# The causal mask of the latent attention as a select on GpSimd, with new orders of work for all engines

## The chip, the cores and the metric

The kernel runs on one core of one Trainium2 chip. The metric is the device time of one execution in microseconds. Before the change it is 1414.62 us, the median of three runs (1412.48 to 1416.68).

## What is computed

The input is 2 x 1024 x 128 (2048 tokens of width 128). The reference is a chain of residual layers; cut to what matters:

```python
x = x + 0.5 * moe0(layernorm(x))        # 8 experts, top 2, capacity, gelu
x = x + attn0(layernorm(x))             # 16 heads of 8, slope bias, causal softmax
x = x + 0.5 * moe0(layernorm(x))
x = x + 0.5 * latent_block(layernorm(x))
x = x + scan_block(layernorm(x))        # conv of 3, tanh, state scan, gelu ffn
x = x + 0.5 * latent_block(layernorm(x))

def latent_block(x):                    # inside: x + attention(rmsnorm(x)) + moe(rmsnorm(.))
    ...
    att = einsum(q, k) / sqrt(D)        # 16 heads of 64: 32 latent + 32 rotary columns
    mask = tril(ones((t, t)))
    att = where(mask, att, -inf)        # no weight on a later key
    att = softmax(att)
```

The change concerns this mask. A masked score becomes a weight of exactly zero after the exponential.

## The kernel before, in words

All tensors are held transposed, features or keys on the 128 partitions and tokens along the free dimension. There are five instruction streams (TensorE, ScalarE, VectorE, GpSimd and SyncE, which issues the DMAs), tied by semaphores, and the program has two large parts: `First` (the first expert layer and the first attention) and `Late` (the second expert layer, then the latent block, the scan block and the latent block again, each for batch element b = 0 and 1).

Attention goes by quads of four heads, n = 0 to 7 in `First` and 0 to 15 in `Late`, and in each quad by two phases ph of 512 queries. For each phase there are these tasks:

- `un` (TensorE, L1269, with the mask constant `maskA` at L1261) makes query-by-key scores, `red` (VectorE, L1544 to L1551) reduces them to row maxima; `m4`, `turn`, `ct` and the DMA `crow` put the maxima into a row of `QS`.
- `sc` (TensorE, `pe_scores`, L1283) makes key-by-query scores minus the maximum in a pair of PSUM banks, 128 keys by 512 queries for two heads at once, in steps listed in `SCORES`. The last five steps of a phase touch the diagonal (`masked`); there, for each piece, two halves of two matmuls (L1290) add -1e30 from the constants `idA` and `maskB` on the diagonal square.
- `exp` (ScalarE, L1461) writes the exponentials of one step, 128 x 1024, into `PR`, a ring of `NPR = 4` group buffers. Two steps make a group; a group is one or two key blocks (`group_pieces`) by four heads.
- `pv` (TensorE, L1383) multiplies a group with the values; it waits for the group's last exponential and frees its buffer for the group four later.
- `ev`, `den`, `ln`, `rx` (ScalarE and VectorE), `on` (GpSimd, L1592) and `proj` (TensorE) normalise and project.

Operands of a later quad are built between the scores: `bld` (TensorE, L1249 to L1251), `bt` (VectorE, L2139), the shuffle `swp` (L2148), the rotation's sums and split `rot` (GpSimd, L2317, L2318, L2320, as one task; quads 0 and 8 do it on the other engines), and a DMA `put`. Norms, routing and experts of a finished half, and for b = 0 also its scan block (the convolution `cv` at L2227 and L2233, products `pct`, `psg`, `pbt` on GpSimd, the scan `scn`), run among the quads of the other half.

The order on each engine is worked out when the program is built. `Plan.simulate` walks through time; whenever an engine is free it takes, among the ready heads of its streams, the task of lowest priority value (`ORDER` for four engines, `WISH` weights for TensorE), charges it `COST`, and notes the order. It also gives out the PSUM banks. What comes out is five fixed lists; on the chip each engine goes through its list and waits on semaphores. So a cost or a weight changes no instruction, only its place and its bank.

Of the kernel before, what the change touches and what calls it, by code (L numbers as in the profile page):

```python
# [102 lines left out]
class Plan:  # L103
# [8 lines left out]
    COST = {"turn": 0.2, "proj": 1.9, "m4": 0.25, "ct": 0.27, "crow": 1.2, "den": 0.72, "ev": 0.58, "ln": 0.63,  # L112
            "rx": 0.63, "on": 1.27, "add": 0.68, "qk": 1.75, "qkh": 1.02, "qkl": 1.22, "val": 1.9, "vc": 1.02, "vs": 0.5,
            "put": 7.0, "egb": 2.7, "exh": 0.6, "exl": 0.69, "ewh": 0.68, "ewl": 0.69, "eu": 1.28, "eg": 0.68, "eh": 0.75,
            "et": 1.3, "ed": 0.87, "eup": 0.75, "mean": 0.87, "cen": 0.69, "sq": 0.63, "var": 0.87, "vln": 0.65, "vex": 0.63,
# [4 lines left out]
    ORDER = {"ACT": ("eg", "rxp", "exh", "ewh", "cmc", "vex", "qkh", "vc", "ev", "exp", "rx", "ln", "vln", "sq"),  # L120
             "DVE": ("ro", "exl", "ewl", "eup", "cen", "eh", "scl", "ct", "m4", "add", "qkl", "red", "den"),
             "POOL": ("vs", "et", "on"),
             "SP": ("crow", "gd", "put", "egb")}

    WISH = {"scm": 2, "unm": 2, "leadm": 4, "upm": 2, "bldm": 2, "sc": 2, "sc1": 1, "un0": 1.9, "un2": 2.89,
# [17 lines left out]
    def quad(self, n, units, values, first_add=(None, None)):  # L143

        add = self.add
        for ph in range(2):
# [8 lines left out]
            for i in range(len(SCORES[ph])):  # L155
# [7 lines left out]
                need = [x]  # L163
# [166 lines left out]
    def simulate(self):  # L330
# [11 lines left out]
        pending = []  # L342
        t = 0.0
        while left:
# [4 lines left out]
            for e in engines:  # L349
# [105 lines left out]
class Late(Plan):  # L455
# [8 lines left out]
        "ve0": 0.63, "scb": 0.49, "ff": 1.27, "xqh": 0.6, "xql": 1.3, "wqh": 1.2, "wql": 1.4, "key": 0.87, "km": 1.4,  # L464
# [51 lines left out]
    @staticmethod  # L516
    def turned(n):
        return ("rotl", n) if n in FAST else ("rot", n)
# [1985 lines left out]
```

## Time and profile before

| | |
|---|---|
| median of three runs | 1414.62 us |
| the profiled execution's own time | 1418.79 us |
| its span, first to last instruction | 1417.0 us |
| TensorE, VectorE | 94%, 71% of the span busy |
| ScalarE, GpSimd | 62%, 28% |
| mean granted clock of TensorE | 0.982 |

The profile is of one execution. The busy time of an engine is the union of its instructions; matmul ends are modelled, so overlapping matmuls count once and the last one's drain counts in full. PE is TensorE, PEld its weight loads, DVE VectorE, ACT ScalarE, POOL GpSimd, SP SyncE. The stages are: load and first expert layer to about 200 us, first attention to 425, second expert layer to 595, the latent and scan blocks to 1417.

### The profile page before, as it was taken

To read this page: it belongs to the slowest core of one execution; us is meant where nothing else is said; L and a number is where in the kernel's file an instruction comes from. 1 tells how busy PE (TensorE), PEld (TensorE's weight loads), DVE (VectorE), ACT (ScalarE), POOL (GpSimd) and SP (SyncE) were. 2 spreads that over 40 slices of the span, in tenths; PEclk is the share of its full clock that TensorE was granted. 3 is DMA by queue.
4 is the path that set the end of the run, shared out by engine and by line. 5 is a ranking of instruction groups with operands and counts; after the bars stand their busy time and mean duration, and the time that the engine had idled before them with its cause. 6 is when DMAs were issued, how large, how long until landed. Compare 5 with 4: busy or idle time off the path is not lost.

```text
span 1417.0 us, 27150 instructions
## 1 busy us (share of the span) xinstructions
PE 1325.2 (94%) x10934; PEld 565.5 (40%) x10934; DVE 1010.7 (71%) x1554; ACT 876.9 (62%) x1124; POOL 394.6 (28%) x317
## 2 busy tenths in 40 slices
PE   7999998989889999989999998989998999999997
PEld 6444333333334444343444343433432334433443
DVE  5444778899915447789887977688878697977635
ACT  5344347788774553366666867766777576675672
POOL 4554420101112555452220332021305033202010
PEclk9999999999999999999999999999998999999998
DMA  6633101000003631011111010010010101101100
GB/s 168 130 61 71 30 9 35 13 2 2 1 1 72 164 60 34 9 24 24 35 24 23 2 24 7 18 35 17 8 23 1 24 12 24 31 8 24 24 2 15
DMA packets 31876, 45.80 MB, mean 32 GB/s; under 512 B 5941, under 2 KB 12789, under 8 KB 31701
## 3 DMA queue, kind: packets, MB, share of 16 engines
q1 hardware_dynamic: 31752, 44.08, 14.7%
q8 instruction: 87, 1.43, 0.4%
q14 instruction: 37, 0.30, 0.1%
HBM read 25.39 MB, written 1.18 MB: 19 GB/s over the span
## 4 chain that ended last, share of the span: by engine, by line
PE 75%; DVE 11%; ACT 8%; issue 4%; DMA 1%; POOL 1%; SPq 0%; ACTq 0%; DVEq 0%; POOLq 0%
PE ps L1283 13%; PE ps L1383 12%; PE ps L1328 8%; ACT PR L1461 6%; PE ps L1249 6%; PE ps L1269 5%; PE ps L1250 5%; PE ps L1251 5%; DVE BM L1551 3%; PE ps L1880 2%; PE ps L1261 2%; PE ps L1347 2%; PE ps L1290 2%; PE ps L1394 2%; PE ps L1395 1%
## 5 line engine op out<-in xcount | busy, mean ns | idle before, releaser
L1461 ACT ACTIVATE PR<-ps 128x1024 f32<-128x1024 f32 x432 | 431.4, 1027 | 204.1 <-PE ps L1290 133.5
L1551 DVE TENSOR_REDUCE BM<-ps 128x2 f32<-128x1024 f32 (+2 forms) x384 | 350.6, 950 | 52.1 <-PE ps L1269 50.7
L1283 PE MATMUL ps<-QS,KS 48*128 48x512 f16 (+7 forms) x2688 | 306.6, 329 | 28.6 <-ACT PR L1461 21.8
L1383 PE MATMUL ps<-PR,VS 128*32 128x512 f32 (+3 forms) x2304 | 232.1, 499 | 2.2 <-ACT PR L1461 1.7
L1283 PEld LDWEIGHTS ps<-QS,KS 48*128 48x128 f16 (+1 forms) x2688 | 108.7, 95 | 199.1 <-ACT PR L1461 87.5
L1269 PE MATMUL ps<-KS,QS 48*128 48x128 f16 (+2 forms) x1728 | 162.6, 274 | 19.0 <-DVE BM L1551 10.9
L1544 DVE TENSOR_REDUCE BM<-ps 128x8 f32<-128x1024 f32 x96 | 116.8, 1220 | 38.7 <-PE ps L1269 37.9
L1269 PEld LDWEIGHTS ps<-KS,QS 48*128 48x128 f16 x1728 | 68.8, 95 | 136.4 <-issue 50.2
L1592 POOL TENSOR_TENSOR OS<-OS,RX 128x512 f32<-128x512 f32 x24 | 31.8, 1327 | 266.9 <-ACT RX L1477 266.9
L1592 POOL TENSOR_TENSOR ON<-OS,RX 128x512 f32<-128x512 f32 x24 | 32.5, 1354 | 260.2 <-ACT RX L1477 260.2
L1249 PE MATMUL ps<-YA,QS 128*128 128x512 f16 x256 | 99.6, 389 | 0.2
L1250 PE MATMUL ps<-YA,QS 128*128 128x512 f16 x256 | 99.3, 388 | 0.0
L1251 PE MATMUL ps<-YA,QS 128*128 128x512 f16 x256 | 99.1, 387 | 0.0
L1418 ACT ACTIVATE BT<-ps 128x512 f32<-128x512 f32 x64 | 38.2, 597 | 95.3 <-PE ps L1251 95.2
L1290 PE MATMUL ps<-maskB,idA 64*128 64x64 bf16 (+1 forms) x1536 | 91.3, 202 | 0.0
L1418 ACT ACTIVATE HL<-ps 128x512 f32<-128x512 f32 x64 | 37.5, 597 | 81.2 <-PE ps L1251 81.1
L1383 PEld LDWEIGHTS ps<-PR,VS 128*32 128x32 f32 x2304 | 53.2, 109 | 80.9 <-issue 63.2
L1290 PEld LDWEIGHTS ps<-maskB,idA 64*128 64x128 bf16 x1536 | 70.3, 94 | 32.8
L1586 POOL TENSOR_TENSOR HL<-HL,PR 128x512 f32<-128x512 f32 x46 | 58.7, 1290 | 57.7 <-DVE HL L1510 45.8
L1547 DVE TENSOR_REDUCE BM<-ps 128x4 f32<-128x1024 f32 x48 | 58.4, 1217 | 6.4 <-PE ps L1269 6.3
L2317 POOL TENSOR_TENSOR KS<-BT,HL 128x1024 f16<-128x1024 f32 x14 | 33.1, 2363 | 87.3 <-DVE HL L2148 87.3
L1261 PE MATMUL ps<-maskA,idA 64*128 64x256 bf16 (+1 forms) x384 | 48.5, 331 | 9.0 <-DVE BM L1551 7.0
(300 smaller groups left out, 2062.0 us busy)
## 6 DMA issues: line engine op xcount, KB each, us to landing
PR<-gates SPq DMA_DIRECT2D x32, 512.0 KB, 13.2
QS<-KS SPq DMA_DIRECT2D x64, 128.0 KB
QS<-KS SPq DMA_DIRECT2D x64, 64.0 KB
WM<-W_in SPq DMA_DIRECT2D x1, 2048.0 KB, 11.7
QS<-HL SPq DMA_DIRECT2D x48, 32.0 KB
KS<-HL SPq DMA_DIRECT2D x48, 32.0 KB
QS<-CT SPq DMA_DIRECT2D x96, 2.0 KB
PR<-x SPq DMA_DIRECT2D x4, 256.0 KB, 4.2
```

The costliest lines, as they stand in the source:

```text
L1249: pe.matmul(dst, w[0], x[0], start=True, stop=False)
L1250: pe.matmul(dst, w[1], x[0], start=False, stop=False)
L1251: return pe.matmul(dst, w[0], x[1], start=False, stop=True)
L1261: pe.matmul(ps[pair][:, w, :].rearrange("p (i c) -> p i c", c=P)[:, :, at_:P], idA[rows, half, :], maskA[rows, half, at_:P].unsqueeze(1).t ...
L1269: ins = pe.matmul(ps[pair][:, w, off:off + nk * P], QS[rows, sl, qt * P:(qt + 1) * P], KS[rows, ks, k0 * P:(k0 + nk) * P], start=not diag, ...
L1283: ins = pe.matmul(ps[pair][:, w, off:off + cols], KS[rows, ks, kt * P:(kt + 1) * P], QS[rows, qs, (ph + 1) * TT - cols:(ph + 1) * TT], sta ...
L1290: ins = pe.matmul(ps[pair][:, w, off:off + wide], idA[rows, half, :], maskB[rows, half, 0:wide], start=False, stop=(half == 1))
L1328: pe.matmul(single(plan, ("ed", 16 * t)), w_out[:, i // 2, i % 2, :], ring_he(lat, u), start=(i == 0), stop=(i == 15)).then_inc(sig["ed"], 1)
L1383: ins = pe.matmul(dst[32 * j:32 * j + 32, TT - cols:TT], v, PR[:, buf, j, off:off + cols], start=(g == 0), stop=(g == NGRP[ph] - 1))
L1461: act.activation(dst, src, ACT.Exp, scale=0.125 if lat else 1.0).then_inc(sig["exp"], 1)
L1544: ins = dve.tensor_reduce(BM[:, ph, p, :, :, 0], bnk[:, :, :].rearrange("a w (i c) -> a w i c", c=P), AX.X, ALU.max)
L1551: ins = dve.tensor_reduce(BM[:, ph, p, :, qt - 4 * ph, part], bnk[:, :, off:off + nk * P], AX.X, ALU.max)
```

## The change

The mask constants stay in use for `First` and for the unit scores. In `Late` the matmuls of L1290 are not issued; instead a new GpSimd task `mk` sets the weights of later keys in the diagonal squares of a masked group to zero, in place in `PR`, and `pv` of such a group waits for it in place of the exponential. The rotation on GpSimd becomes three tasks of one instruction. The plan learns of a port that all GpSimd tasks and the VectorE tasks named in `PORT` pass one after the other. Costs, ranks and weights of both plans are replaced.

```diff
@@ class Plan, costs and weights (First uses these)
-    COST = {... "m4": 0.25, ... "ewh": 0.68, "ewl": 0.69, "eu": 1.28, "eg": 0.68, "eh": 0.75, ... "eup": 0.75,
+    COST = {... "m4": 0.2, ... "ewh": 0.62, "ewl": 0.66, "eu": 1.3, "eg": 0.61, "eh": 0.69, ... "eup": 0.69,
+    PORT = {"exl", "ewl", "scl", "gwl", "mup", "krot", "krl"}
-             "POOL": ("vs", "et", "on"),
+             "POOL": ("et", "on", "vs"),
-    WISH = {... "leadm": 4, ... "un2": 2.89, "qk": -0.24, "vl": 1.91, "proj": 3.84, "bldf": 0.9, "up": 2.16 ...}
+    WISH = {... "leadm": 6, ... "un2": 2.85, "qk": 0.38, "vl": 1.75, "proj": 2.96, "bldf": 0.72, "up": 0.52 ...}
@@ Plan.quad
-                need = [x]
+                cut = self.LATENT and masked(ph, g)
+                need = [add("POOL", "mk", ("mk", n, ph, g), x) if cut else x]
@@ Plan.cost
-                return ((0.66 if self.LATENT else 0.23)
-                        + 0.08 * len(steps) * masked(task[2], group_of_step(*task[2:4])))
+                return 0.66 if self.LATENT else 0.23 + 0.08 * len(steps) * masked(task[2], group_of_step(*task[2:4]))
+        if kind == "mk":
+            return 0.66 * len(group_pieces(*task[2:4]))
@@ Plan.simulate
+                if e == "POOL" or (e == "DVE" and task[0] in self.PORT):
+                    c += max(0.0, port - t)
+                    port = t + c
@@ class Late, costs and weights (all ranks of ORDER are new too)
-        "ksw": ... "bt": 1.22, "rot": 7.0, "lg": 1.1, "dn": 4.9, "cv": 1.3, "dts": 0.9, "scn": 2.3
+        "ksw": ... "bt": 1.22, "rot": 2.36, "lg": 0.98, "dn": 4.6, "cv": 1.95, "dts": 0.68, "scn": 2.4
-             "POOL": ("et", "psg", "pct", "pbt", "xl", "on", "ff", "rot", "xql"),
+             "POOL": ("mk", "pct", "on", "mk", "pbt", "rot", "ff", "xql", "et", "xl", "psg"),
-    WISH = {"scm": 2, "leadm": 4, "upm": 2, "bldm": 2, "un2": 2.1, "lead": 2, "pv3": 2.5, "pv": 3.61, "qk": 0.71,
-            "vl": 1.9, "proj": 3.06, "mean": 1, "bldf": 0.8, "bld2": 3.31, "bld": 1.8, "up": 1.7, "dn": 1.22, ...}
+    WISH = {"scm": 3, "leadm": 3, "upm": 3, "bldm": 3, "un2": 2.39, "lead": 4, "pv3": 0.82, "pv": 2.84, "qk": -1.92,
+            "vl": 8.18, "proj": 9.87, "mean": -0.05, "bldf": -2.69, "bld2": 3.15, "bld": 2.15, "up": -0.36, "dn": 2.88, ...}
@@ Late.builds
-            r = add("POOL", "rot", ("rot", n), r, old)
+            for j in range(3):
+                r = add("POOL", "rot", ("rot", n, j), r, old)
@@ pe_scores
-            diag = masked(ph, group_of_step(ph, i))
+            diag = masked(ph, group_of_step(ph, i)) and not lat
@@ pe_attn, pv
-                pe.wait_ge(sig["exp"], c("exp", n, ph, min(2 * g + 1, LASTS[ph])))
+                if lat and masked(ph, g):
+                    pe.wait_ge(sig["mk"], c("mk", n, ph, g))
+                else:
+                    pe.wait_ge(sig["exp"], c("exp", n, ph, min(2 * g + 1, LASTS[ph])))
@@ pool_attn
+            if task[0] == "mk":
+                n, ph, g = task[1:]
+                pool.wait_ge(sig["exp"], c("exp", n, ph, min(2 * g + 1, LASTS[ph])))
+                for _, off, _ in group_pieces(ph, g):
+                    square = PR[:, group(n, ph, g) % NPR, :, off:off + P]
+                    ins = pool.affine_select(out=square, in_=square, compare_op=ALU.is_ge, fill=0.0, base=0,
+                                             pattern=[[0, QUAD], [1, P]], channel_multiplier=-1)
+                ins.then_inc(sig["mk"], 1)
+                return
```

The second convolution cost of `Late.cost` goes from 1.2 to 1.9. The three instructions of the rotation and their waits are the same as before.

## Rows read from the trace of the kernel before

**Rows 1.** The page, part 1: busy us, share of the span, instructions.

```profile
PE 1325.2 (94%) x10934; PEld 565.5 (40%) x10934; DVE 1010.7 (71%) x1554; ACT 876.9 (62%) x1124; POOL 394.6 (28%) x317
```

**Rows 2.** Windows: length; PE, PEld, DVE, ACT, POOL busy; clock, DMA, GB/s.

```profile
200.00:425.00 225.00, 200.98 (x2305) 78.79 (x2301) 175.12 (x230) 176.00 (x211) 23.18 (x24) 0.98 0.04 9
425.00:595.00 170.00, 166.76 (x667) 73.51 (x667) 93.92 (x143) 73.09 (x111) 86.14 (x69) 0.98 0.32 69
595.00:1417.00 822.00, 765.85 (x7135) 321.25 (x7133) 631.87 (x985) 547.03 (x670) 188.71 (x111) 0.98 0.09 19
595.00:810.00 215.00, 203.04 (x2053) 86.37 (x2052) 182.73 (x285) 145.06 (x180) 60.13 (x34) 0.98 0.11 23
810.00:880.00 70.00, 63.41 (x532) 24.30 (x526) 54.60 (x67) 49.14 (x59) 21.70 (x13) 0.93 0.06 13
1050.00:1120.00 70.00, 63.09 (x498) 24.08 (x496) 50.05 (x61) 50.60 (x62) 21.72 (x12) 0.90 0.09 18
```

**Rows 3.** The chain of waits, 595 to 1377 us: its share by line.

```profile
by line: PE ps L1283 20.4%; PE ps L1383 14.1%; ACT PR L1461 6.0%; PE ps L1269 5.7%; issue 4.6%; DVE BM L1551 3.9%; PE ps L1880 3.0%; PE ps L1249 2.5%; PE ps L1290 2.5%; PE ps L1347 2.2%; PE ps L1261 2.2%; PE ps L1250 2.2%; PE ps L1251 2.1%;
```

**Rows 4.** Waits of PE, 595 to 1377 us: sum us, times, longest.

```profile
PE ps L1283 <- ACT PR L1461: 11.2, 20, 1.1
...
PE ps L1261 <- DVE BM L1551: 6.4, 3, 2.9
```

**Rows 5.** Window 595 to 1417 us of the mask matmuls (L1290) alone.

```profile
595.00:1417.00 822.00, 63.68 (x1024) 47.01 (x1024) 0.98 0.09 19
```

**Rows 6.** Timeline of one diagonal stretch: start us, length us, engine, line.

```profile
1337.90 0.25 PE L1290 MATMUL ps<-maskB,idA 64*128 64x64 bf16 x4
...
1337.98 0.38 PE L1269 MATMUL ps<-KS,QS 48*128 48x512 f16 x2
...
1342.16 0.25 PE L1290 MATMUL ps<-maskB,idA 64*128 64x64 bf16 x4
...
1342.25 0.33 PE L1283 MATMUL ps<-QS,KS 49*128 49x128 f16 x6
...
1342.71 1.02 ACT L1461 ACTIVATE PR<-ps 128x1024 f32<-128x1024 f32 x1 [1.35 <-PE ps L1290]
...
1344.87 1.02 ACT L1461 ACTIVATE PR<-ps 128x1024 f32<-128x1024 f32 x1 [1.13 <-PE ps L1290]
...
1345.19 1.07 PE L1383 MATMUL ps<-PR,VS 128*32 128x384 f32 x16
...
1347.25 0.64 PE L1383 MATMUL ps<-PR,VS 128*32 128x256 f32 x8
```

**Rows 7.** Groups of POOL by form: busy us, mean ns, idle before.

```profile
L2318 POOL TENSOR_TENSOR BT<-BT,HL 128x1024 f32<-128x1024 f32 x14 | 34.8, 2488 | 0.0
L2317 POOL TENSOR_TENSOR KS<-BT,HL 128x1024 f16<-128x1024 f32 x14 | 33.1, 2363 | 87.3 <-DVE HL L2148 87.3
...
L2320 POOL TENSOR_TENSOR KS<-BT,KS 128x1024 f16<-128x1024 f32 x14 | 31.5, 2251 | 1.1
...
L949 POOL TENSOR_SCALAR_AFFINE_SELECT pick<-pick 24x512 bf16<-24x512 bf16 x3 | 2.0, 651 | 0.4
...
L937 POOL TENSOR_SCALAR_AFFINE_SELECT maskB<-maskB 64x256 bf16<-64x256 bf16 x2 | 0.8, 406 | 0.0
```

**Rows 8.** Groups of DVE by form, 595 to 1417 us.

```profile
L2233 DVE SCALAR_TENSOR_TENSOR QS<-QS,colp 128x1023 f32<-128x1023 f32 x4 | 8.4, 2091 | 0.0
...
L2264 DVE SCALAR_TENSOR_TENSOR QS<-QS,colp 128x1024 f32<-128x1024 f32 x2 | 2.5, 1274 | 0.0
```

**Rows 9.** Source view of L1592 (ns min/median/max), timeline of 840 to 850.

```profile
L1592 POOL TENSOR_TENSOR ON<-OS,RX x24: 1264/1274/2241, 216.8 to 1353.7; 128x512 f32<-128x512 f32 x24
...
843.54 2.24 DVE L2233 SCALAR_TENSOR_TENSOR QS<-QS,colp 128x1023 f32<-128x1023 f32 x1
...
844.78 2.98 POOL L2320 TENSOR_TENSOR KS<-BT,KS 128x1024 f16<-128x1024 f32 x1
...
847.72 2.24 POOL L1592 TENSOR_TENSOR ON<-OS,RX 128x512 f32<-128x512 f32 x1
```

More of the change, by code:

```diff
@@ L111 @@
     SINGLES = (4, 5, 6, 7)
-    COST = {"turn": 0.2, "proj": 1.9, "m4": 0.25, "ct": 0.27, "crow": 1.2, "den": 0.72, "ev": 0.58, "ln": 0.63,
+    COST = {"turn": 0.2, "proj": 1.9, "m4": 0.2, "ct": 0.27, "crow": 1.2, "den": 0.72, "ev": 0.58, "ln": 0.63,
             "rx": 0.63, "on": 1.27, "add": 0.68, "qk": 1.75, "qkh": 1.02, "qkl": 1.22, "val": 1.9, "vc": 1.02, "vs": 0.5,
-            "put": 7.0, "egb": 2.7, "exh": 0.6, "exl": 0.69, "ewh": 0.68, "ewl": 0.69, "eu": 1.28, "eg": 0.68, "eh": 0.75,
-            "et": 1.3, "ed": 0.87, "eup": 0.75, "mean": 0.87, "cen": 0.69, "sq": 0.63, "var": 0.87, "vln": 0.65, "vex": 0.63,
+            "put": 7.0, "egb": 2.7, "exh": 0.6, "exl": 0.69, "ewh": 0.62, "ewl": 0.66, "eu": 1.3, "eg": 0.61, "eh": 0.69,
+            "et": 1.3, "ed": 0.87, "eup": 0.69, "mean": 0.87, "cen": 0.69, "sq": 0.63, "var": 0.87, "vln": 0.65, "vex": 0.63,
             "scl": 0.75, "rlg": 4.6, "ro": 0.34, "rxp": 0.31, "rrk": 0.8, "rtp": 0.48, "gd": 0.4, "cmc": 0.6, "cmp": 2.0}
@@ L341, in simulate @@
         left = len(self.needs)
-        pending = []
+        pending, port = [], 0.0
         t = 0.0
@@ L484 @@
-    WISH = {"scm": 2, "unm": 2, "leadm": 4, "upm": 2, "bldm": 2, "sc": 2, "sc1": 1.02, "un0": 1.9, "un2": 2.1,
-            "lead": 2, "un1": 1, "une": 1, "pv3": 2.5, "ahead": 3, "pv": 3.61, "qk": 0.71, "vl": 1.9, "proj":
-            3.06, "ed": 1.1, "mean": 1, "eu": 1.2, "eu1": 0.3, "mode": 0.4, "bldf": 0.8, "bld2": 3.31, "bld":
-            1.8, "up": 1.7, "dn": 1.22, "short": 1}
+    ORDER = {"ACT": ("ev", "eg", "sq", "roth", "krh", "vln", "ewh", "rxp", "sg", "kh", "vex", "si", "ge", "exh", "vc",
+                     "dx", "rex", "exp", "dl", "ve0", "lath", "th", "ab", "ln", "xp", "xh", "de", "xqh", "gwh", "wqh",
+                     "rx"),
+             "DVE": ("ro", "exl", "eh", "gtc", "scl", "den", "cen", "ct", "ewl", "scb", "hf", "krot", "m4", "rt", "eup",
+                     "cv", "dt0", "gt", "mup", "bd", "kl", "oup", "st3", "mya", "cp", "bt", "krl", "wql", "rotl", "dts",
+                     "latl", "fup", "ksw", "swp", "scn", "km", "st2", "add", "rotd", "red", "fya", "gwl"),
+             "POOL": ("mk", "pct", "on", "mk", "pbt", "rot", "ff", "xql", "et", "xl", "psg"),
+             "SP": ("wl2", "egb", "wl1", "crow", "put", "gd", "st", "kput")}
@@ L489, in build @@
+    WISH = {"scm": 3, "unm": 2, "leadm": 3, "upm": 3, "bldm": 3, "sc": 2.04, "sc1": 1.24, "un0": 1.98, "un2":
+            2.39, "lead": 4, "un1": 1.05, "une": 1.17, "pv3": 0.82, "ahead": 3, "pv": 2.84, "qk": -1.92, "vl":
+            8.18, "proj": 9.87, "ed": 1, "mean": -0.05, "eu": 1.13, "eu1": 0.05, "mode": 0.46, "bldf": -2.69,
+            "bld2": 3.15, "bld": 2.15, "up": -0.36, "dn": 2.88, "short": -0.61}
     def build(self):
@@ L2311, in pool_late @@
                 elif kind == "rot":
[L2312 to L2314 removed]
+                    n, j = args
                     b0 = BT[:, 0:2, :]
                     hi, lo = two(STG[:, 0, :]), two(STG[:, 1, :])
[L2317 to L2320 removed]
+                    if j == 0:
+                        pool.wait_ge(sig["swp"], c("swp", n))
+                        put_landed(pool, n - 1)
+                        pool.tensor_tensor(hi, b0, BS, ALU.add).then_inc(sig["rot"], 1)
+                    elif j == 1:
+                        pool.tensor_tensor(b0, b0, BS, ALU.add).then_inc(sig["rot"], 1)
+                    else:
+                        pool.wait_ge(sig["rot"], c("rot", n, 1))
+                        pool.tensor_tensor(lo, b0, hi, ALU.subtract).then_inc(sig["rot"], 1)
                 elif kind == "pct":
```

36 lines of the change are left out of this document (11 added, 25 removed), and 14 rows, old and new, of tables (COST, WISH).

## The prediction

> **What bounds the kernel now.** I read first the page's engine line [rows 1]: TensorE is busy for 1325.2 of 1417.0 us, VectorE for 71%, ScalarE for 62%, GpSimd for 28%. TensorE is the bound on average, so I cut the span into stages [rows 2]. The edit to the computation lives in the latent stage, 595 to 1417 us. There TensorE is busy for 765.85 of 822 us, so it has 56.1 us of idle time; in the first attention (200 to 425) it has 24.0. GpSimd is busy for 188.7 us of the latent stage, 23%. The two 70 us stretches that hold the scan work have a granted clock of 0.93 and 0.90, so part of each ran at 1.2 GHz instead of 2.4.
>
> The chain of waits over 595 to 1377 [rows 3] says what of TensorE is on the path. The mask matmuls (L1290) hold 2.5% of these 782 us, 19.6 us; the scores before them 20.4%, the value products 14.1%, ScalarE's exponentials 6.0%, VectorE's big reductions 3.9%. TensorE's own waits in the stretch [rows 4] are small: 11.2 us for the exponentials, 6.4 for reductions ahead of a unit.
>
> **Part 1, the latent mask matmuls go.** Each latent quad has two phases, each with 8 diagonal pieces (1, 1, 2, 2 and 2 in the last five steps), and a piece has four matmuls: 16 quads x 16 x 4 = 1024, the count of the latent row [rows 5]. That row gives 63.68 us of busy time, 0.25 us a piece, but this counts the modelled drain of each matmul, which the next one overlaps. The timeline [rows 6] has the pace: a mask group starts at 1337.90 and the next work at 1337.98, then 1342.16 to 1342.25. So a piece delays what follows by 0.09 us, and 256 x 0.09 = 23.0 us. The bounds are 19.6 (all that the chain shows) and 63.7 (the whole busy union). I take the pace, since the starts are what the engine gives, and of its 23.0 the 19.6 that were on the path. The rest sits where VectorE or ScalarE came last.
>
> **Part 2, the selects on GpSimd.** Three groups of each phase are masked, with 1, 2 and 1 pieces, so 4 selects over 4 heads x 128 columns: 32 phases x 4 = 128 instructions in 96 tasks. No select of 128x512 f32 is in the trace. Selects of 256 and 512 elements a partition took 406 and 651 ns [rows 7], though the longer is on 24 partitions only. The upper bound is a two-operand step of 128x512, 1.27 us (L1592's median [rows 9]). I take 0.65, the nearest in size and kind; then 83 us are added, and GpSimd is at about 272 of 822 us, 33%. At 1.27 it would be 163 more, 43%. Either way it is no throughput bound; it matters by latency alone.
>
> The latency: the value product (pv) of a masked group now waits for the select, not for the exponential, and on the in-order TensorE everything planned after it waits too. Cover can be read off the timeline [rows 6]. The exponential of the second step of the two-piece group ran 1342.71 to 1343.73, and its pv started at 1345.19: 1.46 us of slack, against 2 x 0.65 = 1.30 plus a hand-over. For the last group the exponential ended at 1345.89 and pv began at 1347.25: 1.36 against 0.65. So even the old order nearly covers it, by the scores and units of the next step; the new plan knows the 0.66 and can put pv later. If cover is gone everywhere, the price is the whole 83 us; if it is perfect, nothing. A second thing is queued behind pv: the exponential of the group four later needs the buffer that it frees; ScalarE has idle time, so a microsecond more there is covered. I take 2 us in all for uncovered selects in the steady run, and 1 us at the very end, where after the last quad's last exponential (about 1371) nothing is left to put ahead of pv. The first half (b = 0) of a layer ends while the other half's quads run, so there it is covered.
>
> **Part 3, GpSimd's queue.** In 14 of 16 quads the rotation occupies it with three steps of 2.36, 2.49 and 2.25 us [rows 7]. Before, they were one task; the edit makes them three of unchanged work, so that a select can be planned between. A select can still come due just as one starts: 42 steps, at worst 2.4 us each, 101 us; at best none, because the plan looks ahead. With 96 tasks in 822 us and 99 us of rotation, chance alone would put 12 selects behind one, with 1.2 us of mean wait, 14 us, less the slack above of at least 0.1 to 0.7. I take 3. The put DMA waits for the third step as before; a select between delays it by 0.65 to 1.3, and a quad's operands are built more than a quad ahead, so that costs nothing; without this cover it would be 14 x 1.3 = 18 us.
>
> There are shared turns too. VectorE's convolution steps with both operands in SBUF took 2.09 us, against 1.27 for a step of equal size with the same kind of operands [rows 8], and beside one of them, begun at 843.54, GpSimd's L2320 took 2.98 instead of a mean of 2.25 [rows 7], and the L1592 behind it 2.24 instead of 1.27 [rows 9]. So the two engines hold each other up when each reads SBUF so. A select is such work; most of VectorE's time is reductions out of PSUM, which went at their 1.22 us regardless. Eight large convolution or scan steps and the few scalings could each catch one: at best nothing, at worst about 20 x 1.3 = 26 us, and I take 2. The Trainium skill (SBUF — State Buffer, the section on two separate sides) says that it is an exclusive lock: whichever starts first blocks the other for the whole instruction. By that rule a select next to a 2 us convolution waits for its end; the trace agrees in kind. The sum changes by nothing, as the stretches in which both occur are 140 of 822 us. The Trainium skill also speaks against the placement (GPSIMD Engine Reference, performance versus the Vector engine): a tight one-input loop over 512 elements takes 769 ns there. By its price the selects would be 98 us instead of 83, and 1.5 for a two-piece group is just over its slack; the trace has 651 ns for 512 elements, and the measured number is the one used.
>
> **Part 4, the plans.** Both orders are made anew: costs near what the trace shows (rotation 3 x 2.36, the convolution 1.95 and 1.9 instead of 1.3 and 1.2), a port that GpSimd and VectorE's listed steps pass one at a time, new ranks and weights. In the latent plan the weights change a lot (three score pairs at once instead of two; projection and values far later); in the first plan little. No row prices an order. What it can give back is TensorE's idle time, 56.1 and 24.0 us, and the lost clock; what it can cost has the same size, as the old order had 11.2 us of waits for exponentials that a poor one would multiply. I take 7 of gain in the latent stage (an eighth of its idle time, mostly around the scans, whose old costs were furthest off) and 1 in the first attention. The expert stages (425 to 595) have TensorE at 98%, so nothing.
>
> **The sum**, against the profiled execution: -19.6 + 3 + 3 + 2 - 8 = -19.6 us. The execution took 1418.79 us (span 1417.0 and 1.8 around it), which is 4.2 above the median 1414.62. So 1399.2 profiled, and 1395 as the median.
>
> **Rivals.** B, the new order gives much: half of the latent and first idle time (40 us), so -19.6 + 8 - 40 = -52, 1363, with a middle at -40, 1375. For it: the old costs missed the scan by a factor of 1.6, and TensorE waited 2.9 us once for a reduction late on VectorE [rows 4]. Against it: most gaps are under 1 us, which no order removes. C, TensorE wasn't last: VectorE is at 182.73 of 215 us in the first latent stretch (85%), and the saved time turns into waits for its reductions. Then about 8 of 19.6 is left and costs of 8 eat it, 1408 to 1416. Against it: over all of 595 to 1377 the chain has VectorE's reductions at 3.9% only. D, on the slower side: selects are late at pv. Place: pv of masked groups, behind a rotation step, or after a select of 1.27 us. Price: up to 83 us of latency. It decides when more than 22.6 of 83 us (the 19.6 and the 8 of the plans, less 5 for queue and turns) show on TensorE, 0.24 us a task; with half exposed the time is 41.5 - 22.6 = 19 longer, 1434. TensorE's waits would also cut its granted clock, as in the scan stretches. Against it: the slack of 1.36 to 1.46 us. E, the change doesn't do what it says, for instance by selects so slow that they serialise, is D at its far end.
>
> **Chances.** Forecast (1385 to 1404) 0.50, B (below 1385) 0.17, C 0.18, D with E 0.15. The measurement tells no change from 0.3%, 4.2 us, so faster means below 1410.4. That holds for the forecast, B and half of C: 0.76. Same: the other half of C, 0.09. Slower: D, 0.15. The range from 1368 to 1419 leaves out the far end of B and most of D, some 0.17. The forecast's own range is 1385 to 1404.
>
> **What would show it.** Right: 512 mask matmuls left, none after 595 us; 128 selects of 0.65 us; hardly a wait of pv (L1383) for GpSimd; ScalarE's wait for mask matmuls turned into one for scores; the latent stage near 803 us and the first attention within 3 of before. Wrong: selects above 1 us, pv waiting for GpSimd for more than 10 us in sum, VectorE's share of the latent chain doubled, a stage before 595 us moved by more than 5, or a granted clock below 0.97.

## The result: 8 us faster, not 20

The forecast was 1395 us. The kernel after takes 1409.99 us in the median (19 runs, 1403.76 to 1415.35), the kernel before 1417.61 in the same comparison: a ratio of 0.994 [0.9925, 0.9954], 0.6%, some 8.5 us. The direction was right. The time lies in the wide range (1368 to 1419) but outside the forecast's own (1385 to 1404), and the size was off by more than half: 8.5 us where I had 19.6. Another 3 us of the distance come from the start, as the median of three that I set out from, 1414.62, was that much too low. The profiled execution took 1408.49 us (span 1406.8), 10.3 less than that of before.

First the page of the kernel after, part 1, which answers to [rows 1]:

```profile
PE 1303.0 (93%) x9910; PEld 535.2 (38%) x9910; DVE 1027.9 (73%) x1554; ACT 854.8 (61%) x1106; POOL 473.8 (34%) x445
```

The 1024 mask matmuls and 22.2 us of TensorE's busy time are gone. The selects are there: GpSimd has 128 instructions and 79.2 us more. VectorE has the same 1554 instructions and 17.2 us more, though the edit adds no work to it; the stretched steps shown further down are the likely reason. Then windows by stage of the kernel after (columns as in [rows 2]):

```profile
200.00:425.00 225.00, 201.29 (x2267) 77.31 (x2263) 173.74 (x229) 176.33 (x211) 23.16 (x24) 0.98 0.04 9
425.00:595.00 170.00, 167.10 (x649) 72.92 (x648) 93.25 (x142) 73.10 (x111) 88.02 (x69) 0.97 0.30 69
595.00:1406.80 811.80, 742.29 (x6126) 293.31 (x6125) 649.75 (x986) 523.57 (x651) 265.83 (x238) 0.97 0.09 19
...
600.00:640.00 40.00, 28.85 (x241) 13.93 (x241) 33.27 (x41) 19.22 (x31) 22.11 (x15) 0.79 0.10 21
1255.00:1280.00 25.00, 18.11 (x119) 6.93 (x119) 21.17 (x37) 9.97 (x14) 9.88 (x7) 0.80 0.00 1
```

This is the view to read. In the latent stage TensorE's busy time fell from 765.85 to 742.29 us, by 23.6, as much as the edit could give. But its idle time, from which I expected a gain of 7, rose from 56.1 to 811.80 - 742.29 = 69.5 us, by 13.4. The difference, 10.2, is all that the stage became shorter. Two short stretches hold much of it: from 600 to 640 TensorE is idle for 11.2 of 40 us, from 1255 to 1280 for 6.9 of 25, and the granted clock is 0.79 and 0.80 there. TensorE's longest waits from 595 to 1380 us in the kernel after (us in total, times, longest), which answer to [rows 4]:

```profile
PE ps L1291 <- ACT PR L1472: 17.1, 28, 1.3
PE ps L1257 <- DVE HL L2228: 5.7, 1, 5.7
PE ps L1400 <- DVE M L1570: 5.5, 1, 5.5
PE ps L1291 <- DVE HL L2228: 4.7, 3, 3.2
...
PE ps L1269 <- DVE CT L1577: 2.2, 1, 2.2
...
PE ps L1394 <- POOL PR L1604: 1.8, 5, 0.9
```

Before, the longest single wait was 2.9 us. Now there are four of 5.7, 5.5, 3.2 and 2.2, together 16.6 us, and all are for VectorE (the M row is the maximum table of a phase, CT its cast, HL an expert's gated product). The value products (L1394, before L1383) waited for a select for 1.8 us only. The source view of the selects (ns, minimum, median, maximum; then who waited for them, in us and times) agrees with the forecast of 0.65 us each and under 10 us of waiting, though only just: weight loads (PEld) waited for 8.1 us more.

```profile
L1604 POOL TENSOR_SCALAR_AFFINE_SELECT PR<-PR x128: 625/635/1128, 603.2 to 1361.4; 128x512 f32<-128x512 f32 x128
...
  PEld ps L1394: 8.1, 16
  PE ps L1394: 1.8, 5
```

The chain of waits by line (595 to 1367 us, kernel after) answers to [rows 3]. The 2.5% of the mask matmuls is gone, "issue" has grown from 4.6 to 7.4% and the value products from 14.1 to 16.8%:

```profile
by line: PE ps L1291 20.7%; PE ps L1394 16.8%; issue 7.4%; ACT PR L1472 6.2%; PE ps L1277 5.7%; PE ps L1900 3.5%; PE ps L1355 2.6%; PE ps L1257 2.1%; PE ps L1405 2.1%; PE ps L1259 1.8%; PE ps L1258 1.8%; PE ps L1269 1.7%; PE ps L1406 1.7%; 
```

The last of the long gaps shows how VectorE was late. The timeline of the kernel after (start, length, engine; [idle before <- releaser]):

```profile
1257.44 2.37 POOL L2338 TENSOR_TENSOR KS<-BT,HL 128x1024 f16<-128x1024 f32 x1
1257.57 2.29 DVE L2083 SCALAR_TENSOR_TENSOR wq<-wq 128x32 f32<-128x32 f32 x1
...
1259.76 2.35 POOL L2340 TENSOR_TENSOR BT<-BT,HL 128x1024 f32<-128x1024 f32 x1
...
1260.11 2.04 DVE L2087 TENSOR_TENSOR wq<-wq,WM 128x32 f32<-128x32 f32 x1
1262.18 2.18 POOL L2343 TENSOR_TENSOR KS<-BT,KS 128x1024 f16<-128x1024 f32 x1
...
1262.63 1.77 DVE L2081 TENSOR_TENSOR wq<-wq,WM 128x32 f32<-128x32 f32 x1
...
1264.55 2.10 DVE L2228 SCALAR_TENSOR_TENSOR HL<-ps,QS 128x512 f32<-128x512 f32 x3
1265.29 0.61 PE L1257 MATMUL ps<-KS,WM 128*128 128x512 f16 x1 [5.67 <-DVE HL L2228]
```

Routing steps of 32 columns, 0.17 to 0.19 us elsewhere, take 1.8 to 2.3 us, and each ends within 0.05 us of the rotation step on GpSimd beside it. The expert product behind them comes late, and TensorE stands. Take, over the whole trace, what each VectorE instruction took beyond the shortest of the same line and form, and add up those parts that are over 0.35 us: this gives 14.1 us before (17 instructions) and 36.8 after (35).

### The profile page after: what moved, and what is told of

Read it like the earlier page. It is cut to its first block, busy times and chain, and to the rows that moved or that the text cites. A ratio compares the mean times of both kernels' runs of the same rounds, so it can differ in the third digit from the quotient of the medians.

```text
span 1406.8 us, 25214 instructions
## 1 busy us (share of the span) xinstructions
PE 1303.0 (93%) x9910; PEld 535.2 (38%) x9910; DVE 1027.9 (73%) x1554; ACT 854.8 (61%) x1106; POOL 473.8 (34%) x445
## 4 chain that ended last, share of the span: by engine, by line
PE 72%; DVE 9%; ACT 9%; issue 6%; SPq 1%; POOL 1%; DMA 1%; ACTq 0%; DVEq 0%; POOLq 0%
PE ps L1291 13%; PE ps L1394 12%; PE ps L1336 8%; ACT PR L1472 6%; PE ps L1257 5%; PE ps L1277 5%; PE ps L1259 5%; PE ps L1258 5%; PE ps L1900 3%; PE ps L1355 2%; DVE BM L1562 2%; PE ps L1405 2%; PE ps L1269 2%; PE ps L1351 2%; PE ps L1406 1%
## 5 line engine op out<-in xcount | busy, mean ns | idle before, releaser
L1291 PE MATMUL ps<-QS,KS 48*128 48x512 f16 (+7 forms) x2688 | 294.7, 329 | 39.6 <-ACT PR L1472 28.8
L1394 PE MATMUL ps<-PR,VS 128*32 128x512 f32 (+3 forms) x2304 | 236.6, 504 | 6.4 <-ACT PR L1472 3.9
L1291 PEld LDWEIGHTS ps<-QS,KS 48*128 48x128 f16 (+1 forms) x2688 | 114.0, 95 | 219.1 <-ACT PR L1472 95.2
L1604 POOL TENSOR_SCALAR_AFFINE_SELECT PR<-PR 128x512 f32<-128x512 f32 x128 | 81.8, 654 | 310.8 <-ACT PR L1472 310.8
L1394 PEld LDWEIGHTS ps<-PR,VS 128*32 128x32 f32 x2304 | 52.6, 110 | 96.8 <-issue 69.5
L1597 POOL TENSOR_TENSOR RX<-RX,PR 128x512 f32<-128x512 f32 x26 | 34.2, 1325 | 46.7 <-DVE RX L1521 23.5
L1336 PE MATMUL ps<-HL,WM 128*128 128x512 f32 x92 | 46.1, 604 | 0.0
```

The costliest lines, as they stand in the source:

```text
L1291: ins = pe.matmul(ps[pair][:, w, off:off + cols], KS[rows, ks, kt * P:(kt + 1) * P], QS[rows, qs, (ph + 1) * TT - cols:(ph + 1) * TT], sta ...
L1336: pe.matmul(single(plan, ("ed", 16 * t)), w_out[:, i // 2, i % 2, :], ring_he(lat, u), start=(i == 0), stop=(i == 15)).then_inc(sig["ed"], 1)
L1394: ins = pe.matmul(dst[32 * j:32 * j + 32, TT - cols:TT], v, PR[:, buf, j, off:off + cols], start=(g == 0), stop=(g == NGRP[ph] - 1))
L1597: pool.tensor_tensor(ring_he(lat, u), ring_he(lat, u), GB[:, t % 2, i // 2, :], ALU.mult).then_inc(sig["et"], 1)
L1604: ins = pool.affine_select(out=square, in_=square, compare_op=ALU.is_ge, fill=0.0, base=0, pattern=[[0, QUAD], [1, P]], channel_multiplier=-1)
```

## The experiments

Fourteen kernels. "Before" was run beside them each time, at 1418 to 1420 us, so kernels of different comparisons are set against each other by their ratios to it; 0.1% is 1.4 us. Where two ratios are subtracted, the interval takes them as independent, and comes to 3 to 5 us for most pairs, so that a smaller difference is not clear of noise. Each trace is of one execution.

**1 and 2. The mask both ways, in the new orders.** The kernel after with its orders kept; in the first the latent mask is made by matmuls again, in the second by both.

```diff
-            diag = masked(ph, group_of_step(ph, i)) and not lat
+            diag = masked(ph, group_of_step(ph, i))
@@ the first alone: pv waits for "exp" again, and POOL's "mk" task does nothing
```

> The changed kernel with every order kept as it is, but the latent mask done by the mask matmuls again: no select is issued and pv waits for the exponential. So only the computation edit is undone. Against the changed kernel's 1410 us: theory A (the edit saved what its pace says, about 20 us, and the new orders lost part of it elsewhere) expects 1427 to 1433, that is 9 to 15 above the kernel before. Theory B (the mask matmuls cost far less than 0.09 us a piece) expects at most 1418. Theory C (late selects ate the gain) expects 1410 or less, since the selects' waits go too.

> The changed kernel, same orders, with mask matmuls added and the selects kept, so a piece is masked twice. Its distance to the changed kernel is the price of the matmuls, its distance to the run with matmuls alone the price of the selects. Theory A expects 1427 to 1433, within 3 us of the run with matmuls alone; B at most 1418; C 8 us or more above the run with matmuls alone.

Measured: 1.0007 [0.9985, 1.003] with matmuls alone, 1.0046 [1.0018, 1.0074] with both. So the new orders without the edit give nothing, +1.0 us (+-3.2), where I had -8. The matmuls cost 1.0046 - 0.994, 15.0 us (+-4.5), and the selects 1.0046 - 1.0007, 5.5 us (+-5.1). The time with matmuls alone was as theory B has it, the one with both lies between A and B. TensorE's waits in the kernel with matmuls alone (595 to 1385 us):

```profile
PE ps L1397 <- DVE M L1567: 5.5, 1, 5.5
PE ps L1257 <- DVE HL L2218: 4.8, 1, 4.8
```

These are two of the long gaps of the kernel after, and the other two (3.2 and 2.2 us) are there too. So the gaps belong to the new order and not to the selects.

**3. The edit alone, planned anew with the old costs and weights.**

```diff
@@ class Late of before: COST, ORDER, WISH, rotation and port as they were
-                need = [x]
+                cut = self.LATENT and masked(ph, g)
+                need = [add("POOL", "mk", ("mk", n, ph, g), x) if cut else x]
```

> The kernel before with the mask edit alone: selects on GpSimd, planned at 0.66 us each and first in GpSimd's ranks; all other costs, ranks, weights and the one-task rotation as before, no port in the plan. Theory A expects 1396 to 1402 (before less 15 to 21), since in this order only few of the rotations fall into VectorE's routing steps; B expects 1412 to 1418; C 1418 or more, as a select can't come between the three rotation steps.

Measured: 1434.45 us, 1.0107 [1.0084, 1.013], 15 us slower than before. The planner, given one more task, found another order throughout. Its windows row of the latent stage (to be read against [rows 2]):

```profile
595.00:1434.70 839.70, 766.48 (x6092) 296.73 (x6089) 632.04 (x981) 540.73 (x664) 269.33 (x238) 0.95 0.09 18
```

TensorE is as busy as with the mask matmuls, 766.48 us, though 1024 instructions are gone; its clock was granted at 0.95 instead of 0.98, and it is idle for 73.2 us. Theory A missed by over 30 us. The time is in C's range, but nothing here tests C's reason, as the whole order differs. So "the edit alone" means little where a planner reorders: the order must be held.

**4. Four rotations moved.** In the new latent order the rotations of quads 6, 10, 14 and 15 run beside routing chains. They were put behind later selects.

```diff
+    for n, after in ((6, ("mk", 4, 0, 2)), (10, ("mk", 8, 0, 2)), (14, ("on", 12, 0)), (15, ("mk", 13, 0, 2))):
+        move(plan.order["POOL"], [("rot", n, j) for j in range(3)], after)
```

> The changed kernel with one reordering on GpSimd: the rotations of quads 6, 10, 14 and 15 go behind the selects that follow them, which takes them out of VectorE's routing steps; nothing else moves. Theory A, in the form that rotations hold the port while VectorE's small two-operand routing steps wait, expects VectorE's lengthened routing steps (5 to 7 us at two places, 3 at two more) gone, TensorE's waits of 3.2 and 5.7 us for the step behind them gone, and 1397 to 1403. Rival: TensorE's waits are due to VectorE's queue as such and come back elsewhere; then 1407 to 1413.

Measured: 0.9943 [0.9927, 0.9959], as the kernel after and as the rival has it. The gaps of 5.67 and 3.24 us went, two of 3.73 came. The timeline of this kernel has rotation 6 in its new place:

```profile
790.20 2.36 POOL L2357 TENSOR_TENSOR BT<-BT,HL 128x1024 f32<-128x1024 f32 x1
790.33 2.27 DVE L2119 CAST wq<-wq 128x32 bf16<-128x32 f32 x1
792.64 2.17 POOL L2360 TENSOR_TENSOR KS<-BT,KS 128x1024 f16<-128x1024 f32 x1
792.86 1.99 DVE L2119 CAST wq<-wq 128x32 bf16<-128x32 f32 x1
```

It now stretches two casts near the end of the same chain. This collision had been moved, not removed.

**5. The missing corner: selects in the old order.** PE, ACT, VectorE and SyncE keep the order of before instruction for instruction; only GpSimd gets the selects, each where its exponential ends in the plan.

```diff
+def add_selects(plan):
+    at = {}
+    for x in plan.order["POOL"]:
+        if x[0] == "rot":
+            at.update({x + (j,): plan.start[x] + 2.4 * j for j in range(3)})
+        else:
+            at[x] = plan.start[x]
...
+                    at["mk", n, ph, g] = plan.seen["exp", n, ph, min(2 * g + 1, len(SCORES[ph]) - 1)]
+    plan.order["POOL"] = sorted(at, key=at.get)
```

> The orders of PE, ACT, VectorE and SyncE are those of before, instruction for instruction; the latent mask is made by selects, each put into GpSimd's old order where its exponential ends in the plan, the matmul masks are gone, and the rotation is three tasks as in after. It is the missing corner of four: old order with matmul masks 1417.6, new order with matmul masks 1418.4 (ratio 1.0007), new order with selects 1410.0 (0.994). Theory A (the computation edit is worth its 9 to 10 us at any fixed order, and the plans nothing): 1407 to 1411, ratio about 0.994. Theory B (the new plans are what makes room for the selects; in the old order they come late behind rotations and et): 1416 to 1430, with PE's wait for selects over 20 us. The kernel planned anew with the old weights took 1434, which B would read as the edit's own cost and A as the replanning's.

Measured: 0.9963 [0.9945, 0.9981], between the two theories: 5.2 us (+-2.6) from the edit at the old order. Its value products waited for selects longer than in the new order (source view; L1620 is the select):

```profile
  PEld ps L1410: 15.5, 18
  PE ps L1410: 6.8, 10
```

**6. The stretched weight-split steps moved.** Between 606 and 627 us four of VectorE's weight-split steps took 1.35 to 2.44 us beside rotations, instead of 0.28.

```diff
+    for c in range(5):
+        move(plan.order["DVE"], [("gwl", c)], ("red", 1, 1, 4 + c))
```

> After's kernel with one thing moved: the 5 weight-split steps of VectorE (two instructions each), 4 of which were stretched from 0.28 us to 1.35 to 2.44 us beside GpSimd's rotation near 606 to 631 us, stand between the later reductions of quad 1 instead. Theory A (the stretched steps cause the 5.46 and 2.16 us gaps of TensorE at 618.8 and 624.6, and the low clock of 0.50 to 0.59 behind them): both gaps go below 1.5 us and the time falls by 6 to 10 us, to 1400 to 1404. Theory B (one collision is exchanged for another, as when the rotations were moved): the gaps come back within 30 us of there, and the time stays within 2 us of after, 1408 to 1412.

Measured: 0.9935 [0.9911, 0.9959], no change. The steps are short again, and the gap of 5.46 us is still there, to the hundredth (source view, then TensorE's waits from 600 to 640):

```profile
L2233 DVE SCALAR_TENSOR_TENSOR WM<-WM x10: 210/277/518, 645.1 to 651.9; 128x128 f16<-128x128 f32 x8, 128x64 f16<-128x64 f32 x2
...
PE ps L1417 <- DVE M L1587: 5.5, 1, 5.5
```

My theory of this gap fell: three of the stretched steps stand ahead of VectorE's wait for the late eviction, and take nothing that it wouldn't have waited. The fourth, at 624.15 us, stood ahead of a cast, and the gap of 2.16 us behind it went down to 0.4. The stretch from the last row-maxima cast before it (at 579 us) to this one took 45.39 us instead of 47.17. Such a 1.8 us is too little for the times to show.

**7. And the last rotation.** The kernel of 6 with the rotation of quad 15 alone moved.

```diff
+    move(plan.order["POOL"], [("rot", 15, j) for j in range(3)], ("mk", 13, 0, 2))
```

> After's kernel with the weight-split steps moved as in the run before and only the last rotation (of quad 15) moved behind the select of quad 13's first phase; rotations 6, 10 and 14 stay. Its move took away the 5.67 us gap at 1259.6 without a new one near it in the run with four rotations moved. Theory A (gaps and the clock behind them are what took back the gain): another 6 to 8 us below the run before, 1394 to 1398. Theory B (what is saved in a gap is lost in a later wait): 1406 to 1412, with the last norm and routing chains, not the middle, setting the end.

Measured: 1404.18 us, 0.9891 [0.9872, 0.991], by the ratios 6.2 us (+-4.3) below 6, between the two theories. But two gaps of 6 are missing in the trace of 7: the one of 5.66 us, and one of 3.25 us at 996 us, next to which nothing was moved. The row-maxima casts (the CT rows of VectorE) tell them apart, since the stretch between two of them mostly repeats to hundredths of a microsecond where the order is the same. Across the first gap it fell from 35.92 us (1250.59 to 1286.51) to 30.85 (1244.52 to 1275.37), by 5.1; across the second from 25.55 to 20.89, by 4.7. So the rotation of quad 15 is worth some 5 us, and the second gap's part in that trace is luck. The other three rotations were not moved one at a time.

**8. No turns on the port in the planner.**

```diff
-                    c += max(0.0, port - t)
```

> After's kernel, but the planner charges no turns on the port that GpSimd and VectorE's two-operand steps share; weights, costs, selects and the three-part rotation stay, and the orders are planned anew from them (its own planned end moves from 947.6 to 976.8). Theory A (the charge is what makes the new order good): VectorE's stretched steps rise from 36.8 us to over 45 and the time to 1425 to 1440. Theory B (an order found anew differs by chance, and the charge as such keeps no collision away): stretched steps stay at 30 to 40 us, and the time is anywhere from 1410 to 1435, as the kernel with old weights was (1434).

Measured: 1441.46 us, 1.0163 [1.0141, 1.0185]. But VectorE's stretched time, by the sum used above, is 19.1 us, less than the kernel after has, not more, which neither theory expected. So in this pair the turns as such didn't keep collisions away. The order is another one throughout; TensorE is busy for 768.1 of 845.1 us from 595 on, and it has other waits, among them:

```profile
PE ps L1276 <- DVE BM L1561: 10.0, 12, 1.8
...
PE ps L1290 <- DMA QS<-CT: 4.9, 2, 3.3
PE ps L1404 <- DVE BM L1561: 4.3, 1, 4.3
```

**9. VectorE's order at the 5.46 us gap.** In the kernel after, just before that gap ended:

```profile
617.54 0.73 DVE L1581 STREAM_SHUFFLE RX<-OS 128x512 f32<-128x512 f32 x1
618.16 1.21 DVE L1562 TENSOR_REDUCE BM<-ps 128x2 f32<-128x1024 f32 x1
619.28 2.35 DVE L2159 SCALAR_TENSOR_TENSOR BT<-ps,WM 128x1024 f32<-128x1024 f32 x2
621.54 1.22 DVE L1562 TENSOR_REDUCE BM<-ps 128x2 f32<-128x1024 f32 x1
...
623.92 0.19 DVE L1570 TENSOR_REDUCE M<-BM 128x16 f32<-128x48 f32 x1
```

VectorE had stood for an eviction at 617.54, and then did two latent products (L2159) and a swap for quad 2 ahead of the table (L1570) that TensorE needed. These three steps, 3.6 us, were put behind it.

```diff
+    move(plan.order["DVE"], [("bt", 2, 0), ("bt", 2, 1), ("swp", 2)], ("ct", 0, 1))
```

> The kernel of the run with the split and the last rotation moved, and three VectorE steps of quad 2 (its two latent products and their swap, 3.6 us together) moved from ahead of the last reduction and maximum table of quad 0's second phase to behind that table's cast. The 5.46 us gap of TensorE near 621 us was not caused by the stretched steps (it stayed at 5.46 when these were moved): VectorE stood 5.8 us for an eviction and then did these three first. Theory A (the order of VectorE makes the gap): the gap falls from 5.46 to about 1.9 us and the time by 3 to 4 us, from 1404.2 to 1400 to 1401. Theory B (TensorE would wait for the moved steps instead, since quad 2's rotation comes 3 us later): a new gap within 40 us of there, and no change, 1403 to 1406.

Measured: 1399.65 us, 0.9866 [0.9845, 0.9888], 3.5 us below 7 by the ratios, which is not clear of noise (+-4.1). The trace shows it: the gap is 2.09 us, near the 1.9 worked out, and the stretch between the casts around it took 41.87 us instead of 45.37, 3.5 less. It is 41.0 to 41.9 in all four kernels with this edit. (The trace also has a gap of 3.24 us at 773 us that 7 doesn't have, and the stretch around it is 4.6 us longer; no edit stands next to it.) Timeline of this kernel:

```profile
618.26 0.72 DVE L1600 STREAM_SHUFFLE RX<-OS 128x512 f32<-128x512 f32 x1
618.88 2.34 DVE L1581 TENSOR_REDUCE BM<-ps 128x2 f32<-128x1024 f32 x2
...
621.60 0.27 PE L1419 MATMUL ps<-identf,M 128*16 128x128 f32 x1 [2.09 <-DVE M L1589]
```

**10. And the old first attention.** Class First gets the costs, ranks and weights of before, and no port turns.

```diff
 class First(Plan):
+    COST = {"turn": 0.2, "proj": 1.9, "m4": 0.25, ...}   # with LAND, ORDER and WISH, as before
...
-                if e == "POOL" or (e == "DVE" and task[0] in self.PORT):
+                if self.LATENT and (e == "POOL" or (e == "DVE" and task[0] in self.PORT)):
```

> The same kernel, but the first attention and first experts run in the order of before (its costs, weights and no port turns); the latent stage is unchanged. From the first row maxima cast to the last of the first attention before took 241.4 us in the profiles and the new order 243 to 244; my forecast had the new order 1 us faster there. Theory A: another 1 to 3 us, 1398 to 1400. Theory B (what the first attention gains is waited for at the second router or in the expert stage): no change, within 1 us of the run beside it.

Measured: 1396.28 us, 0.9842 [0.9822, 0.9863], 3.4 us below 9 by the ratios, again not clear of noise (+-4.2). This is the fastest kernel, 13.9 us (+-3.6) below after by the ratios and 22 below before. The traces settle the sign. From the first row-maxima cast to TensorE's last long wait in the first attention (3.57 us, at 414 to 421 us) it is 264.65 us in six of the seven traces with the old first order and 266.3 in the seventh; in the eight with the order of after it is 267.7 to 269.0. So the new first order cost some 3 us, where I had it at -1.

**11. Wide selects.** The same result, 96 of the 128 selects 256 keys wide.

```diff
-                    square = PR[:, group(n, ph, g) % NPR, :, off:off + P]
+                    wide = min(2 * P, width)
+                    square = PR[:, group(n, ph, g) % NPR, :, off:off + wide]
```

> After's kernel with 96 of the 128 selects 256 instead of 128 keys wide: the same result, and GpSimd's time in selects grows by 96 x 0.5 = 48 us in the same places of the same orders. It doubles the suspected cost of the selects (their length ahead of the value products, and the time in which GpSimd may hold the shared port). Theory A (the selects cost TensorE about 5 us by their length at the few value products that wait, as the run with both masks gave): the time rises by another 4 to 8 us over after, to 1414 to 1418, PE's wait for selects from 10 to over 16 us. Theory B (they are covered, and the 5 us were the new order's): within 2 us of after, 1408 to 1412.

Measured: 1.0011 [0.9992, 1.003], 10 us (+-3.4) slower than after, as theory A has it, for 43.6 us more on GpSimd (517.4 busy). Source view of the selects:

```profile
L1605 POOL TENSOR_SCALAR_AFFINE_SELECT PR<-PR x128: 629/1061/1557, 602.6 to 1366.9; 128x1024 f32<-128x1024 f32 x96, 128x512 f32<-128x512 f32 x32
...
  PEld ps L1394: 17.5, 30
  PE ps L1394: 7.6, 15
```

At 0.65 us the selects just fit their slack of 1.3 to 1.5 us [rows 6]; at 1.06 two in a row don't. The price isn't all in the last row, which grew by 5.8 us (from 1.8); where the rest goes wasn't followed up.

**12. Both masks in the old order.** Kernel 5 with the diff of 2.

> The old orders with the selects put in, and the matmul masks kept as well: the mask is made twice, nothing else differs from the run with old orders and selects (0.9963 of before). In the new order the same pair gave 15 us for the matmuls and 5.5 for the selects, so 9.5 net; in the old order only 5.3 net is known. Theory A (the matmuls were partly hidden in the old order, whose TensorE waits more often for VectorE): this comes to 1.004 or less, so the matmuls cost 8 to 11 us there and the selects 4 to 6. Theory B (the matmuls cost their 15 us everywhere, and the selects cost more where no plan made room for them): 1.007 to 1.010, selects 10 to 14 us.

Measured: 1.0046 [1.0029, 1.0062]. In the old order the matmuls cost 11.8 us (+-3.5) and the selects 6.5 (+-2.4), much as in the new one, and each a little over theory A's figures.

**13 and 14. The matmul mask in the fastest order.** Kernel 10 with the mask by matmuls; in 14 the rotation of quad 15 is held by another task, as no select is there to hold it.

```diff
-    move(plan.order["POOL"], [("rot", 15, j) for j in range(3)], ("mk", 13, 0, 2))
+    move(plan.order["POOL"], [("rot", 15, j) for j in range(3)], ("on", 13, 0))
```

> The order of the fastest kernel so far (0.9842 of before: new latent order with the split, the last rotation and the three look-up steps moved, old first attention), with the latent mask by matmuls and without selects. Theory A (the edit is worth the more, the fewer waits the order leaves, since a microsecond taken from TensorE counts only where TensorE is last): the time is 11 to 15 us above the kernel with selects, 1407 to 1411 or 0.992 to 0.995. Theory B (it is worth 9 to 10 us in the new order whatever is repaired): 1405 to 1406.5, 0.991. If it is 0.985 or less, the repairs had made the matmuls free and the fast time was theirs.

> The run before (repaired order, matmul mask), with the rotation of quad 15 behind the normalisation of quad 13's first phase on GpSimd. Without selects nothing held the rotation where it had been moved to: it began at 1261.95 us, ran beside a routing chain, and TensorE stood 4.82 us again at 1265. Theory A (10 of the 15.3 us are the edit's, 5 the rotation's return): the 4.82 us gap is gone and the ratio is 0.990 to 0.992, 1404 to 1407.5; the edit is then worth 8 to 11 us in the repaired order as in the new one. Theory B (the edit is worth 13 us or more where few waits are left): the gap is gone, but the ratio stays at 0.993 or more.

Measured: 0.995 [0.9928, 0.9972] and 0.9879 [0.9856, 0.9902]. The number of 13 met theory A by luck: the rotation's gap was back and took its part. By the ratios 14 is 10.1 us (+-4.5) faster than 13, where I had 4 to 7. In the traces two gaps went, the 4.82 us of the rotation and one of 3.24 at 773 us, which neither edit touches. The same stretch in both kernels, 13 first (from the start of its gap), then 14:

```profile
1265.00:1290.00 25.00, 18.32 (x152) 7.41 (x154) 20.70 (x36) 11.78 (x15) 5.06 (x3) 0.80 0.00 1
```

```profile
1260.00:1285.00 25.00, 23.30 (x227) 8.50 (x227) 19.74 (x27) 14.47 (x17) 8.04 (x4) 0.93 0.01 1
```

From the table cast before the gap to the one behind it 13 took 36.5 us and 14 took 29.8: a gap of 4.82 us cost 6.7. Around the gap of 3.24 it was 26.0 against 21.4, 4.6 us. Both cost 1.4 times their length. The granted clock is low behind them, 0.80 against 0.93 at the first and 0.86 against 1.00 at the second (773 to 798 us in 13, 765 to 790 in 14), and matmuls of 0.38 us take 0.63 there. And the gap of 3.24 comes and goes without an edit. It is there in kernel 10:

```profile
765.71 2.12 POOL L2381 TENSOR_TENSOR KS<-BT,KS 128x1024 f16<-128x1024 f32 x1
765.72 2.16 DVE L2121 SCALAR_TENSOR_TENSOR wq<-wq 128x32 f32<-128x32 f32 x1
...
768.53 1.46 PE L1329 MATMUL ps<-QS,KS 49*128 49x384 f16 x12 [3.25 <-DVE HL L2266]
```

and not in 14, with the same instructions in the same order on VectorE and in the rotation:

```profile
769.46 2.19 POOL L2371 TENSOR_TENSOR KS<-BT,KS 128x1024 f16<-128x1024 f32 x1
769.46 0.19 DVE L2111 SCALAR_TENSOR_TENSOR wq<-wq 128x32 f32<-128x32 f32 x1
```

In 10 the routing step ended with the rotation's third step, in 14 it went through beside it. The starts don't tell why: GpSimd's is ahead by under 0.01 us in both. So which way such a tie falls is open, and as each kernel has one trace, it isn't known how many of its executions have the gap. (The profiled execution of 13, 1419.01 us, was one of its slowest; they ran from 1402.96 to 1419.16.) Kernel 14 is 5.2 us (+-4.4) slower than 10, and in the traces 10 had this gap and 14 had not. From the first row-maxima cast of the latent stage to the last, 10 took 748.24 us and 14 took 754.33, 6.1 more; the stretch with the gap was 4.3 us longer in 10. Neither theory of 14's expectation held as written; that the edit is worth some 10 us there, with equal gaps, rests on this sum and not on a run of its own.

## Why the forecast was wrong

The parts as measured in the new order add up to the result: matmuls -15.0, selects 5.5, orders 1.0, in all -8.5, where I had -19.6, +8 and -8. (The three come from four kernels' ratios, so they must add up; what they show is the shares.)

1. **The step that failed is part 4, the plans at -8.** With matmuls the new orders cost 1.0 us (+-3.2), with selects they gave 3.3 (+-3.3, after against kernel 5). I priced them as a share of TensorE's idle time, and said myself that no row prices an order. The idle time rose by 13.4 us. What the order cost can be named place by place, from the stretches between casts: VectorE's order around 620 us (kernel 9, 3.5 us), a stretched weight-split step beside it (kernel 6, 1.8), the rotation of quad 15 inside a routing chain (kernel 7, some 5), and the first attention (kernel 10, some 3). Together they are about 13 of the 13.9 us (+-3.6) that lie between after and kernel 10; of the single steps the times show only that of kernel 7 clear of noise, and a gap of 3 us that came and went is mixed into it. How much an order can be worth kernels 13 and 14 show, whose mask is made by matmuls as before: 0.995 and 0.9879, 7 and 17 us.
2. **Part 1, the mask matmuls at 19.6, was too high by a quarter or more**: 15.0 and 11.8 in two orders. The pace of 0.09 us a piece [rows 6] was read in two places where TensorE had no wait; over 256 pieces it is 0.046 to 0.059. The share in the chain of waits [rows 3], which I took for the part on the path, charges an instruction for its place in the chain, not for what its absence gives: in kernel 5, which is kernel 12 without the matmuls, TensorE was busy for 1303.2 instead of 1323.9 us, 20.7 less, but idle for 104.1 of its span instead of 97.4, 6.7 more. So in this pair a third of the busy time that goes comes back as waiting, which is rival C in small; in the kernel after, the waits of scores for exponentials went from 11.2 us to 17.1.
3. **Parts 2 and 3, the selects at 8 in all, were right within the noise**: 5.5 (+-5.1) and 6.5 (+-2.4) measured; 635 ns against 0.65 us; 1.8 us of waits on TensorE's matmuls and 8.1 on its weight loads. Kernel 11 shows that this was close: at twice the width the edit is worth nothing.
4. **The shared turns at 2 were looked for in the wrong place.** I asked what the selects would do to the convolution and scan steps. What cost in the gap at 1259 us was the old work, the rotation, beside the routing steps: small instructions that I hadn't counted, as their busy time is nothing. The Trainium skill (SBUF — State Buffer, the section on two separate sides) says that a VectorE instruction with two SBUF inputs and one of GpSimd that reads SBUF take a shared pair of ports in turns, each for its whole instruction; by that a step of 0.17 us can wait 2.3, and the rows at 1257 us agree.
5. **The rivals.** C's range, 1408 to 1416, held the time, and half of its mechanism: the waits were VectorE's, but in four gaps of 2.2 to 5.7 us and not for reductions all along, and with the other terms as measured its number is partly luck. B (the orders give much) was wrong for this order; kernel 10 shows that there was room. D did not come. Of the signs that I named, the select's length, the few waits and, within the 5 us named, the stages before 595 us came as written; the first attention, 3.2 us longer than before by the measure used for kernel 10, was just outside the 3 that I had named, and the latent stage at 811.8 instead of 803 spoke against the size. The clock sign, below 0.97, did not come: 0.97 in that stage, 0.978 over the span.

What stays open: why the edit gave 5.2 us (+-2.6) in the old order and 9.5 (+-3.8) in the new one. The intervals overlap, and a gap of 3 us came and went between kernels with the same order around it. Kernel 10 still has the rotation of quad 6 beside routing; a better place for it wasn't tried.

## What to carry to other kernels

Price an edit by holding the order of everything else; a planner that is run again is a second, larger change (here -3, +20 and +28 us against the old order, with the same selects: kernels after, 3 and 8 against 5). Where a change is smaller than the noise of the times, compare the same stretch in two traces, from one small instruction to a later one: where the order is the same it mostly repeats to hundredths. Read an order's worth from single gaps: list each wait over 2 us of the bounding engine, follow it to the engine that was late, and look at what that engine did first, and whether tiny steps there took ten times their usual length. Don't price what an instruction's absence gives by its share of the chain alone: here it gave 0.6 and 0.8 of it (11.8 and 15.0 of 19.6 us), in a stage where VectorE was busy for 77% of the time.

## What the runs showed of the hardware

- A select of 128x512 f32 on GpSimd took 635 ns in the median (625 the shortest), one of 128x1024 about 1.06 us (kernel 11).
- VectorE instructions with operands in SBUF only, a plain cast of 32 columns among them, took up to 2.3 us instead of 0.17 beside a GpSimd instruction of 2.36; reductions out of PSUM beside such an instruction kept their 1.21 us. With starts within 0.01 us of each other, the same pair took 2.16 and 2.12 us in one kernel and 0.19 and 2.19 in another.
- TensorE's granted clock was 0.80 over the 25 us from the start of a 4.82 us gap, and 0.93 over the like stretch without it, and the gap cost 1.4 times its length.
